# Ranking rounds inside the pipeline's steps, and a rewritten drain, in a recommender block on one Trainium2 core

## What is computed

```python
# token stage: three table rows for each id, three gelu branches, fused, layer-normed
cat = concat(gelu(emb[id] @ w_item + b), gelu(geo[id] @ w_geo + b), gelu(visit[id] @ w_visit + b))
h = emb[id] + 0.1 * (layer_norm(gelu(cat @ w_fuse + b)) * (id != 0))
# attention over the 128 tokens of a sequence, 4 heads of 16
h = h + attention(layernorm(h))
# routed feed-forward: in each sequence only the 63 tokens of the largest weight take part
x3 = layernorm(h)
weights = x3 @ wr + br                         # one number for each token
sel = top_k(weights, 64)[:63]                  # the 63 largest; equal ones by position
y = gelu(x3 @ w1 + b1) @ w2 + b2               # for the chosen tokens
out = h + x3 + where(chosen, weight * y, 0)    # written in float32, 4.19 MB
```

## Time and profile before

| | |
|---|---|
| median of 3 timed runs | 551.7 us (551.21 to 551.77) |
| profiled execution | 550.62 us, its span 548.8 us |
| PE matmul | 460.9 us (84%), 5850 instructions |
| DVE | 420.1 us (77%), 1648 instructions |
| ACT | 378.3 us (69%) |
| POOL | 350.4 us (64%) |
| mean granted clock of PE | 0.946 of full speed |

### The profile page before, as it was taken

One profiled execution on the slowest core, in us unless ns is written; L12 is line 12 of the kernel. 1 busy time (PEld: TensorE's weight loads), 2 busy tenths in 40 slices (PEclk: granted clock), 3 DMA queues, 4 the chain that ended last, 5 costly groups with the idle time before them and its releaser, 6 DMA issues. The chain is left out here.

```text
span 548.8 us, 16472 instructions
## 1 busy us (share of the span) xinstructions
PE 460.9 (84%) x5850; PEld 340.7 (62%) x5850; DVE 420.1 (77%) x1648; ACT 378.3 (69%) x662; POOL 350.4 (64%) x412
## 2 busy tenths in 40 slices
PE   5778889898988998889898989988899989967760
PEld 2445567676666666666666666666677766756550
DVE  1368689777778888887777787888777778878386
ACT  1235678788777777778787877777787877837350
POOL 5756666676676676667666766666676677431573
PEclk9889899999999999999999999999998999979555
DMA  3112101111111111011111111111111111000046
GB/s 97 31 28 34 23 12 21 26 23 23 23 23 23 21 17 17 16 21 23 23 23 23 23 23 18 17 17 18 23 23 23 23 23 24 1 2 4 19 127 161
DMA packets 23733, 15.72 MB, mean 29 GB/s; under 512 B 18848, under 2 KB 21536, under 8 KB 23712
## 3 DMA queue, kind: packets, MB, share of 16 engines
q0 software_dynamic: 6144, 9.97, 11.8%
q1 hardware_dynamic: 17568, 5.48, 3.7%
HBM read 10.98 MB, written 4.19 MB: 28 GB/s over the span
## 5 line engine op out<-in xcount | busy, mean ns | idle before, releaser
L335 POOL TENSOR_TENSOR rs<-ve,minus_half 128x4 f32<-128x4 f32 x96 | 104.0, 1093 | 66.0 <-DVE ve L677 63.7
L327 POOL DMA_INDIRECT G<-table,idx x64 | 66.1, 1033 | 53.8 <-issue 43.6
L770 DVE TENSOR_REDUCE neg_max<-psum 128x4 f32<-128x512 f32 x128 | 84.2, 679 | 1.9 <-PE psum L1124 1.7
L327 POOL DMA_INDIRECT G<-turned,idx x64 | 60.7, 948 | 19.5 <-issue 19.2
L1052 PE MATMUL psum<-wt,hid 128*128 128x64 f32 x512 | 67.4, 287 | 2.2 <-ACT hid L471 1.4
L464 ACT ACTIVATE prob<-psum 128x512 f32<-128x512 f32 x128 | 66.1, 603 | 4.2 <-PE psum L1094 2.4
L1052 PEld LDWEIGHTS psum<-wt,hid 128*128 128x128 f32 x512 | 63.6, 202 | 3.4 <-ACT hid L471 2.3
L664 DVE BATCH_NORM_STATS2 st<-psum 128x6 f32<-128x64 f32 x128 | 19.9, 218 | 37.3 <-PE psum L1219 30.3
L508 ACT ACTIVATE x2t<-psum 128x256 f32<-128x256 f32 x32 | 12.3, 385 | 46.5 <-PE psum L1174 46.5
L464 ACT ACT_TABLE_LOAD x31 | 39.8, 1283 | 4.3 <-PE psum L1094 3.8
L1124 PE MATMUL psum<-k_s,q_s 32*128 32x128 f32 x1024 | 39.3, 291 | 4.1 <-ACT prob L464 3.9
(11 more groups left out here) (116 smaller groups left out, 1100.6 us busy)
## 6 DMA issues: line engine op xcount, KB each, us to landing
out<-R SPq DMA_DIRECT2D x13, 256.0 KB, 2.7
G<-table,idx POOLq DMA_INDIRECT x64
G<-turned,idx POOLq DMA_INDIRECT x64
wt<-packed SPq DMA_DIRECT2D x1, 932.0 KB, 5.0
q_s<-max_t SPq DMA_DIRECT2D x32, 8.0 KB
out<-R SPq DMA_DIRECT2D x1, 512.0 KB, 4.1
out<-R SPq DMA_DIRECT2D x2, 128.0 KB, 3.5
ids_sb<-ids SPq DMA_DIRECT2D x1, 64.0 KB, 1.8
```

Source lines behind the costliest of these rows:

```text
L327: pool.indirect_dma_start(G[par][:, b, :], None, turned if b >= 2 else table, bass.IndirectOffsetOnAxis(ap=idx[par][:, b:b + 1], axis=0),) ...
L335: pool.tensor_tensor(rs[:, :], ve[:, :], minus_half[:, :], ALU.pow).then_inc(S[dst], 1)
L770: dve.tensor_reduce(neg_max[:, GB * h:GB * h + GB], bank[h].rearrange("p (b k) -> p b k", b=GB), AX, ALU.max, negate=True).then_inc(S["max ...
```

## The change

1. `pipeline` gets an `end`. DVE and PE leave their loops behind step 17 (`SPLIT = 18`), so that steps 18 to 29 are straight code on these two; POOL, ACT and SP keep their loops.
2. Part 0 of the ranking is now the first 64 sequences and goes into those steps: PE's `weights_t(0)` in step 18 behind the projection, DVE's `take_weights(0)` behind `masked`; one round in each of steps 19 to 25 behind `keys_out`; `select(0)` in step 26; `coefficients(0)` and `take_coef(0)` in step 27.
3. Part 1 is sequences 64 to 119. Its rounds are spread over the drain.
4. The last eight sequences (groups 30 and 31) are not ranked by rounds. PE's `wide` writes the weight of each token of a sequence over all partitions, DVE's `compare` counts how many are larger (or equal and earlier) and takes the token if there are fewer than 63. `lower` is a triangle of ones made in the setup (two more DVE instructions).
5. Group 31 gets its routed part straight from PSUM (`shift_routed`, `finish`), the rest by `add_routed` in new pieces: ten on POOL, the first in step 29 and the others between its drain steps, six on DVE, five of which ACT scales. SP stores in a new order, 17 stores in place of 16.
6. PE has five matmuls of 256 columns that nothing reads (`keep_busy(2 * P, 5)`), three ahead of `coefficients(1)` and two behind `x3_t(31)`. ACT loads its tables at other places and copies the maxima of group 31 before the values of group 30.

Its core (constants, POOL, ACT, DVE, PE):

```diff
+HALF = P // 2
+TAIL = P - 2 * GB
+PARTS = ((0, HALF), (HALF, TAIL))
+SPLIT = 18
+SUMS = tuple((n, 8) for n in range(0, TAIL, 8)) + ((TAIL, GB),)
+ACT_SCALED = (8, 9, 10, 11, 14)
+POOL_SUMMED = (0, 1, 2, 3, 4, 5, 6, 7, 12, 13)
+DVE_SUMMED = (8, 9, 10, 11, 14, 15)
+STORES = POOL_SUMMED[:8] + (8, 9, 12, 10, 11, 13, 14, 15)
+LAST = (P - GB, GB)
...
+                last = type(i) is int and i == NG - 3
+                if last:
+                    weighted(d)
+                    add_x3(d)
+                    add_routed(0)
...
             rstd(ve3, rs3, "ve3_ready", "rs3_ready", NG - 3)
             weighted(NG - 3)
             add_x3(NG - 3)
-            pool.wait_ge(coef_ready, 1)
-            wait(pool, "y_ready", 1, TAIL // GB - 1)
-            add_routed(0)
+            add_routed(3)
+            add_routed(4)
...
             x3_out(NG - 3)
+            maxima_out(NG - 1)
             values_out(NG - 2)
-            load_for_ffn()
-            maxima_out(NG - 1)
...
             x3_out(NG - 1)
-            scale_routed(2)
+            scale_routed(8)
             hidden(NG - 1, 0)
             hidden(NG - 1, 1)
-            scale_routed(3)
+            scale_routed(9)
+            scale_routed(10)
+            scale_routed(11)
+            scale_routed(14)
...
+            def compare(g):
+                dve.wait_ge(wide_ready, g - TAIL // GB + 1)
+                for b in range(GB):
+                    wide, own = bank[RANK_BANK[g]][:, b * P:(b + 1) * P], wb[g % 2][:, b:b + 1]
+                    last = dve.scalar_tensor_tensor(equal[:, b, :], wide, own, lower[:, :],
+                                                    ALU.is_equal, ALU.mult)
+                done(last)
+                for b in range(GB):
+                    wide, own = bank[RANK_BANK[g]][:, b * P:(b + 1) * P], wb[g % 2][:, b:b + 1]
+                    last = dve.scalar_tensor_tensor(above[:, b, :], wide, own, equal[:, b, :],
+                                                    ALU.is_gt, ALU.add)
+                done(last)
+                done(dve.tensor_reduce(rank[:, :], above[:, :, :], AX, ALU.add))
+                dve.scalar_tensor_tensor(of(coef, g), rank[:, :], float(KEEP), wb[g % 2][:, :],
+                                         ALU.is_lt, ALU.mult).then_inc(rank_done, 1)
...
                 if on(b):
                     keys_out(b, odd)
+                if type(i) is int and SPLIT < i <= SPLIT + KEEP // 8:
+                    rounds(0, i - SPLIT - 1, i - SPLIT)
+                if type(i) is int and i == SPLIT + KEEP // 8 + 1:
+                    select(0)
...
                 if on(a):
                     masked(a)
+                if type(i) is int and i == SPLIT:
+                    take_weights(0)
+                if type(i) is int and i == SPLIT + KEEP // 8 + 2:
+                    take_coef(0)
...
-            pipeline(dve, step, ahead=3)
+            pipeline(dve, step, ahead=3, end=SPLIT)
...
             center(c3, of(R, NG - 2), mv3, "c3_ready", NG - 2)
+            rounds(1, 1, 3)
             ffn_out(NG - 3)
-            route(NG - 3)
-            take_coef(0)
             norm3(NG - 2)
+            rounds(1, 3, 5)
 
             sums(NG - 1)
             divide(NG - 1)
+            rounds(1, 5, 6)
             attention_out(NG - 1)
             route(NG - 2)
+            with_bias(NG - 2)
+            rounds(1, 6, KEEP // 8)
             residual(NG - 1)
             sums3(NG - 1)
             means(st3, mv3, "st3_ready", "mv3_ready", NG - 1)
             variances(mv3, ve3, "mv3_ready", "ve3_ready", NG - 1)
             center(c3, of(R, NG - 1), mv3, "c3_ready", NG - 1)
-            wait(dve, "r_ready", 1, TAIL // GB - 1)
-            add_routed(0)
-
+            select(1)
             norm3(NG - 1)
+            take_coef(1)
...
+            compare(NG - 2)
+            add_routed(8)
+            compare(NG - 1)
+            shift_routed(NG - 1)
+            add_routed(9)
+            finish(NG - 1)
...
                 if on(e):
                     project(e)
+                if type(i) is int and i == SPLIT:
+                    wait(pe, "v_out", 1, b)
+                    weights_t(0)
+                if type(i) is int and i == SPLIT + KEEP // 8 + 2:
+                    wait(pe, "v_out", 1, b)
+                    coefficients(0)
                 if on(d):
                     ffn_second(d)
+                if type(i) is int and i == SPLIT:
+                    pe.wait_ge(rank_in, 1)
+                if type(i) is int and i == SPLIT + KEEP // 8 + 2:
+                    pe.wait_ge(coef_ready, 1)
...
-            pipeline(pe, step)
+            pipeline(pe, step, end=SPLIT)
             scores(NG - 2, 0)
             wait(pe, "c1_ready", 1, NG - 1)
             values_of(NG - 3, 0)
-            weights_t(0)
             x2_t(NG - 1)
...
             project(NG - 1)
+            wait(pe, "o_t_ready", 1, NG - 1)
+            wide(NG - 2)
             ffn_second(NG - 2)
 
+            for n in range(3):
+                keep_busy(2 * P, 5)
+            coefficients(1)
             x3_t(NG - 1)
-            weights_t(1)
+            for n in range(2):
+                keep_busy(2 * P, 5)
             ffn_first(NG - 1)
+            pe.wait_ge(coef_ready, 2)
+            wide(NG - 1)
             ffn_second(NG - 1)
-            coefficients(1)
```

184 lines of the change are left out of this document (104 added, 80 removed).

## The result

The changed kernel took 547.8 us (median of 8 runs, 543.3 to 560.2), the one before 553.3 us beside it (median of 8, 548.7 to 559.9). The ratio is 0.9893, 95% interval 0.9856 to 0.9931: 1.1% faster, where 538.0 us, 2.5% less, had been forecast. The range ended at 546.0, so the median lies outside it, close to rival A's 548. The ratio is taken from the fast runs alone.

What follows compares the result with a forecast made beforehand. No engine was full: DVE's loop handling, 1.0 us a step, lay on the step's cycle, and the last stores' release set the end. 548.8 - 7.1 - 6.3 - 0.1 = 535.3 us span, hence 538.0 us; range 532.5 to 546.0.

Steps and rivals of the forecast that it cites:

- rival A: Steps 18 to 27: loops kept on POOL or ACT hold the 15.24 us pace, only the drain gains: 548; chance 0.12.
- Part 1: Steps 18 to 27 straight on DVE and PE: 14.2 us a step instead of 15.24, bounds 14.0 and 15.24.
- Part 2: Ranking of the first 64 sequences inside steps 18 to 27: adds 3.3 us, leaving ten steps 7.1 us shorter.
- Rival D: Fetching the straight code of ten more steps makes the kernel slower than before, up to 559; chance 0.03.
- Part 3: Drain from W of step 29 to x3 of group 31: 6.3 us earlier; 8.4 at full clock, 4.0 at half.
- Part 4: x3 of group 31 to the store burst: 10.85 us against 10.98, nothing gained or lost, bounds -1.5 and +7.
- rival C: Comparisons of the last groups: STTs slow beside POOL, 7 us more, 545; chance 0.06.
- Part 5: From the release of the last eight stores to the end: 11.4 us as before.

Runs made afterwards that it cites:

- e3: The kernel before, with only DVE written as straight code from step 18: 530.12 us in a single run, steps 18 to 25 at 14.21 us.
- f1: The changed kernel with POOL too straight from step 18, ACT and SP still looped: 536.1 us, ratio 0.968 to the kernel before.
- f2: The changed kernel with ACT and SP too straight from step 18, only POOL looped: seven of steps 18 to 25 at 14.88 us.
- f3: The kernel before, with only POOL straight from step 18: 538.76 us in a single run, against 551.1.
- h2: The changed kernel with POOL straight from step 18 but keeping its semaphore increments: 14.81 to 14.90 us in five of steps 18 to 25.
- e6: e5 with one ranking round in place of seven, so other tokens are chosen: steps 20 to 25 at 14.14 us against 14.23.
- e5: The changed kernel with all five engines straight from step 18 and pieces 12 and 13 stored ahead of 9: 531.05 us, ratio 0.9546 to the kernel before.
- e9: The changed kernel itself, run once more beside its variants: 546.4 us, ratio 0.984 to the kernel before.
- e4: The changed kernel with pieces 12 and 13 stored ahead of 9, and 8 ahead of 7: 523.6 us, ratio 0.981 to the kernel before.
- e2: The kernel before, with only POOL straight from step 18: 532.56 us in a single run, steps 18 to 25 at 14.38 us.

## Why the prediction was wrong, point by point

**Part 1 is the step that failed.** "So the loop's own handling on DVE costs 0.76 + 0.25 = 1.0 us a step" took a gap on DVE for DVE's. It costs 0.27 us (e3), and of the gap's 0.76 only 0.1 is DVE's. The other 0.65 is the stall, which goes when POOL leaves its loop and doesn't when the others do (f1, f2, f3). So the pitch fell from 15.13 to 14.98 us and not to 14.2. The 152.4 us of the ten steps also hold the long step 25, 1.0 us that the prediction spread over all ten. The argument against rival A, that the gap is on DVE with the release already there, was no argument: DVE stood before an instruction that had its inputs, but so did PE between two matmuls, and the cause was on a third engine. The one row that could have warned was named in the prediction, too: in step 28 POOL had become straight as well. Rival A named the right engine for a reason that is shown in part only, gathers with "issue" gaps, and its chance of 0.12 was too small. That its 548 was nearly the measured time is luck: by its own sum the ten steps cost 3.3 us more than before and the drain gains 6.4, a span of 545.7. The ten steps cost 0.7 more and the drain behind W of step 29 gained 3.2, the span was 547.6, and the median lay 1.6 us below the profiled execution and not 1.1 above it.

The Trainium skill's rule on the fetch of code behind a taken branch (Runtime: NRT & Kernel Launch, "Instruction fetch mechanics") does not explain the stall: there is one branch in two steps and a stall in each, and h2 has the stall without a branch on POOL.

**Part 2.** A round costs 0.1 us a step and not 0.24 (e6 against e5, seven rounds 0.7 us against 1.7). `select` costs 0.3 us (14.55 against 14.24) and not 0.6; steps 18 and 27 cost nothing that shows (14.16 and 14.17 in e5). That is 1.0 us instead of 3.3. In e5, with all loops left, the ten steps took 142.5 us where 142.0 + 3.3 had been forecast: the base of 14.2 us a step was right, but it needs POOL out of its loop, and the ranking was priced too high. Of the 7.8 us that the changed kernel's ten steps took above the forecast, 4.4 are the pitch and 3.4 the two long steps, 25 and 27.

**Rival D** did not happen: e5 has 30 packets of instructions in q8 as well, all five engines straight, and steps of 14.23 us.

**Steps 28 and 29** were to stay as they were. Step 28 took 15.65 us, right behind the dip of the clock that ends at 459; in e5, without that dip, it took 14.11. Step 29 took 13.30: POOL's `xw` and add of x3 stand earlier in the new order, and DVE's `rm` and `s`, which ran beside them before, took 0.16 and 0.43 us in place of 0.58 and 0.92.

**Part 3.** x3 of group 31 was forecast 34.0 us behind W of step 29, between 31.9 at full and 36.3 at half clock. It stood at 36.3 in the profiled execution, where the clock was 0.68 from 490 to 500 us and at half from 507 to 516, at 32.4 in e9, and at 30.8 in e4 and e5 at full clock (40.3 before). So it came out on its half-clock bound, with stretches of half clock in it. The term was the right one, its bounds were too narrow: over all runs with the new drain the stretch was 30.8 to 37.2 us (37.2 in e6 and f1).

**Part 4.** 12.9 us against 10.85. The price of the comparisons was right (0.28 against 0.27 for each); rival C is out. Two terms were mis-sized: a comparison of a group takes 3.4 to 3.6 us with its reduction (0.69) and the pauses between, not 3.0; and the two TTs of `shift_routed` 2.6 us, not 0.85. They were priced as with POOL idle, in the very paragraph that says both-SBUF instructions are slow beside it. The two adds of 512 elements took 0.69 us each instead of 1.1 and gave 0.8 back.

**Part 5.** 10.3 us from the release, not 11.4. The last sum was ready 16.2 us behind x3 here and 18.2 before, which may be why; no run tests it. But 2.2 us were lost ahead of the release, with the DMA engines idle behind SP's wait (e4). The prediction took the order of the stores as given and never compared it with the order in which the pieces become ready.

The span then closes: 535.3 + 7.8 (steps 18 to 27) + 0.9 (28 and 29) + 2.3 (part 3) + 1.0 (parts 4 and 5) + 0.4 (step 17 itself was later) = 547.7, and the span is 547.6.

## What to carry to other kernels

A gap on an engine that has its inputs says where the time is lost, not who loses it: before pricing an engine's loop, find a stretch in which that engine alone has left it, or make one. Here the engine to take out of its loop first was the one that issues the indirect gathers: with the stall, one line on POOL alone took 6.3 us out of ten steps (f3), where the whole change was worth 5.5 us of time; without it, 1.0 us (e2). And put the stores in the order in which their pieces become ready, since one wait of the issuing engine holds all that is behind it.
